# Searching the last 18 adjacency tiles of a sparse graph attention layer: other units, and a plan in two batches

## The reference

```python
h = jnp.maximum(_layernorm(x), 0.0)                  # x: 6144 x 512
h = jnp.einsum('ni,hif->hnf', h, W)                  # 8 heads of 64
s1 = jnp.einsum('hnf,hf->hn', h, a1)
s2 = jnp.einsum('hnf,hf->hn', h, a2)
scores = leaky_relu(s1[:, :, None] + s2[:, None, :], 0.2)
scores = jnp.where(adj[None] > 0, scores, -9e15)     # adj: 6144 x 6144 int32, 0 or 1
out = jnp.einsum('hnm,hmf->hnf', softmax(scores), h)
return x + elu(out as 6144 x 512)
```

## Time and profile before

| | |
|---|---|
| median of 3 runs | 793.66 us (792.19 to 800.2) |
| the profiled execution | 800.12 us, of it span 798.2 us |
| mean granted TensorE clock | 0.848 |
| DVE busy | 659.8 us, 83% |
| PE matmul busy | 570.5 us, 71% |
| ACT busy | 469.2 us, 59% |
| POOL busy | 424.6 us, 53% |
| mean DMA rate | 338 GB/s |

### The profile page before, as it was taken

The page is one execution under the profiler, slowest core; times in us unless marked ns, Lnnn a source line. Parts: engine busy times, 40 slices in busy tenths (PEclk is TensorE's granted clock), DMA queues, the critical chain, the costliest instruction groups (busy, mean ns, idle before and its releaser), DMA issues.

```text
span 798.2 us, 9153 instructions
## 1 busy us (share of the span) xinstructions
PE 570.5 (71%) x2182; PEld 407.3 (51%) x2182; DVE 659.8 (83%) x2066; ACT 469.2 (59%) x695; POOL 424.6 (53%) x804
## 2 busy tenths in 40 slices
PE   0389789898877777653777677677767669988770
PEld 0255445554444444342566465556655558766560
DVE  4659988999886767764879998999979989999871
ACT  0777797799999989324265655666455123333231
POOL 4634444443442432227666466647675776888720
PEclk9989999999998989855879879686887769997895
DMA  9999988899999999418989999999998888999986
GB/s 287 423 365 384 349 330 341 338 378 420 419 422 419 419 419 424 196 40 312 389 325 410 414 402 387 406 395 410 392 405 282 216 239 231 284 279 277 285 236 160
DMA packets 65130, 269.51 MB, mean 338 GB/s; under 512 B 12145, under 2 KB 12145, under 8 KB 52786
## 3 DMA queue, kind: packets, MB, share of 16 engines
q1 hardware_dynamic: 32098, 177.95, 55.5%
q0 software_dynamic: 26368, 78.36, 32.3%
q10 hardware_dynamic: 6608, 12.58, 4.2%
HBM read 243.49 MB, written 25.37 MB: 337 GB/s over the span
## 4 chain that ended last, share of the span: by engine, by line
DVE 20%; PE 16%; issue 10%; ACT 3%; another core or an unknown queue 3%; DMA 1%; POOL 1%; POOLq 0%; DVEq 0%; ACTq 0%
DVE nodes L1122 7%; PE psP L1260 5%; PE psP L1261 4%; DVE places L250 3%; PE psP L1267 3%; PE psP L1268 3%; DVE best L239 2%; ACT packed L229 2%; PE psC L1244 2%; DMA nodes<-table,list_column 1%; DVE agg L1134 1%; POOL nodes L959 1%; DVE to_row L1092 1%; DVE result L1142 1%
## 5 line engine op out<-in xcount | busy, mean ns | idle before, releaser
L651 PE MATMUL psH<-sb_W,normedT 128*128 128x512 f32 x384 | 222.5, 671 | 0.0
L229 ACT ACTIVATE packed<-adj_rows,eight 128x3072 uint8<-128x3072 int32 x66 | 188.5, 2856 | 3.8 <-DMA adj_rows<-in_adj_dram 3.2
L954 POOL DMA_INDIRECT nodes<-table,column x138 | 138.5, 1003 | 68.4 <-issue 39.5
L1260 PE MATMUL psP<-nodes,ident 128*128 128x256 f32 x276 | 107.8, 480 | 53.0 <-issue 40.1
L959 POOL DMA_INDIRECT nodes<-table,list_column x109 | 110.8, 1017 | 64.2 <-DVE list_column L1081 33.6
L1122 DVE TENSOR_TENSOR nodes<-nodes,psW 128x2048 f32<-128x2048 f32 (+4 forms) x66 | 138.7, 2142 | 5.1 <-ACT psW L1029 5.0
L698 POOL TENSOR_TENSOR sb_node_sum<-sb_node_sum,h_rows 128x512 f32<-128x512 f32 x48 | 61.1, 1273 | 141.4 <-ACT h_rows L616 141.4
L652 PEld LDWEIGHTS psS<-sb_Wa,normedT 128*128 128x128 f32 x384 | 78.1, 203 | 101.8 <-issue 101.8
L250 DVE FIND_INDEX8 places<-best,packed 128x8 uint32<-128x96 f32 (+6 forms) x240 | 110.4, 468 | 0.0
L239 DVE MAX8 best<-packed 128x8 f32<-128x96 f32 (+6 forms) x240 | 103.2, 463 | 4.5 <-ACT packed L229 4.5
L1261 PE MATMUL psP<-nodes,ident 128*128 128x264 f32 x276 | 104.5, 467 | 0.0
(11 more groups left out here) (177 smaller groups left out, 925.0 us busy)
## 6 DMA issues: line engine op xcount, KB each, us to landing
adj_rows<-in_adj_dram SPq DMA_DIRECT2D x66, 1536.0 KB
sb_adj_rows<-in_adj_dram SPq DMA_DIRECT2D x30, 1536.0 KB, 12.7
table<-h_rows SPq DMA_DIRECT2D x48, 260.0 KB, 8.7
sb_x_rows<-in_x_dram SPq DMA_DIRECT2D x48, 256.0 KB, 8.9
result<-in_x_dram POOLq DMA_DIRECT2D x19, 512.0 KB
out_dram<-result ACTq DMA_DIRECT2D x19, 512.0 KB
result<-in_x_dram POOLq DMA_DIRECT2D x10, 256.0 KB
out_dram<-result ACTq DMA_DIRECT2D x10, 256.0 KB
```

The lines of the kernel that those rows point to most:

```text
L229: nc.scalar.activation(words.bitcast(mybir.dt.uint8), sb["adj_rows"][buffer_of(i)][:], ACT.Square, bias=sb["eight"][:], scale=-17.0, accum ...
L651: nc.tensor.matmul(psH[:, t % 2], normedT[:, t % 2, kc], sb["W"][:, kc], start=(kc == 0), stop=(kc == KC - 1))
L954: nc.gpsimd.indirect_dma_start(out=nodes[:, node_at[u] + i * w.direct + j], out_offset=None, in_=table, in_offset=bass.IndirectOffsetOnAxi ...
L1260: nc.tensor.matmul(low, sb["ident"][:], nodes[:, n, 0:LOW], start=a, stop=False)
```

## The change

The searches move to other rounds, and the late tiles are counted and placed in two batches.

- A tile is searched whole in one round, as before, but rounds of units with ten blocks are left out. The rounds are 0 to 5, 7 to 13 and 17 to 21: tiles 30 to 35 stay where they were, tiles 36 to 42 come one round later (7 to 13), tiles 43 to 47 come four rounds later (17 to 21). ACT packs in the round before: tiles 30 to 35 as before, nothing in round 5, tile 36 in round 6, tile 37 in 7 and so on to tile 42 in round 12, nothing in 13, 14 and 15, tile 43 in round 16 up to tile 47 in round 20.
- Batch 0 is tiles 30 to 37: `count_late(0)` in round 9, `place_late(0)` at the end of round 10. Batch 1 is tiles 38 to 47: `count_late(1)` in round 22, `place_late(1)` in round 23.
- `look_up(u)` waits for the first `late_planned` where u > 12, for the second where u > 25.

```diff
     late = next(u for u, w in enumerate(UNITS) if w.tile >= EARLY)
-    COUNTED = late - 6
+    later = next(u for u, w in enumerate(UNITS) if w.tile >= SPLIT)      # SPLIT = 38
     dve_items = [(t, n) for t in range(EARLY, TILES) for n in range(2 * len(segments_of(t)))]
-    dve_round = spread_over([scan_cost(*item) for item in dve_items], COUNTED)
+
+    searchers = [u for u in range(later - 6) if UNITS[u].blocks < WIDEST]
+    dve_round = [searchers[t - EARLY] for t, _ in dve_items]
...
+    batches = [(EARLY, SPLIT, E, E + SPLIT - EARLY, scanned_in[SPLIT], late), (SPLIT, TILES, E + SPLIT - EARLY, V, later - 6, later)]
+    assert batches[0][4] <= late - 6
...
-                if u == late:
-                    pool.wait_ge(late_planned, 1)
+                for b, batch in enumerate(batches):
+                    if u == batch[5]:
+                        pool.wait_ge(late_planned, b + 1)
...
-                if u == COUNTED:
+                if u == later - 6:
                     rank_last(nc, dve, sb, TILES - 1)
-                    count_late()
-                if u == COUNTED + 1:
-                    place_late()
+                for b, batch in enumerate(batches):
+                    if u == batch[4]:
+                        count_late(b)
+                    if u == batch[4] + 1:
+                        place_late(b)
...
-                if u > COUNTED + 3:
-                    pe.wait_ge(late_planned, 1)
+                planned = sum(u > batch[4] + 3 for batch in batches)
+                if planned:
+                    pe.wait_ge(late_planned, planned)
...
-                if u == COUNTED:
-                    pe.wait_ge(late_counted, 1)
+                for b, (_, _, v0, v1, counted, _) in enumerate(batches):
+                    if u != counted:
+                        continue
+                    pe.wait_ge(late_counted, b + 1)
                     pe.wait_ge(facts_done, u + 4)
-                    nc.tensor.matmul(psC[:, 0:LV], sb["earlier"][:], listed[:], start=True, stop=True)
-                    nc.tensor.matmul(psC[:, LV:2 * LV], sb["ones"][:], listed[:], start=True, stop=True).then_inc(late_placed, 1)
+                    n, mine = v1 - v0, slice(v0 - E, v1 - E)
+                    nc.tensor.matmul(psC[:, 0:n], sb["earlier"][:], listed[:, mine], start=True, stop=True)
+                    nc.tensor.matmul(psC[:, n:2 * n], sb["ones"][:], listed[:, mine], start=True, stop=True).then_inc(late_placed, 1)
```

More of the change, by code:

```diff
@@ L42 @@
 INFO = 2 + 2 * H
+SPLIT = 38
 GROUP = 1024
@@ L849, in attend_edges @@
     E = next(k for k, v in enumerate(VISITS) if v.tile >= EARLY)
-    LV, E0 = V - E, E - FIRST["C"]
+    LV = V - E
+    batches = [(EARLY, SPLIT, E, E + SPLIT - EARLY, scanned_in[SPLIT], late), (SPLIT, TILES, E + SPLIT - EARLY, V, later - 6, later)]
+    assert batches[0][4] <= late - 6
     def ring(size):
@@ L982, in square @@
                 w = UNITS[u]
-                if u == late:
-                    act.wait_ge(late_planned, 1)
+                for b, batch in enumerate(batches):
+                    if u == batch[5]:
+                        act.wait_ge(late_planned, b + 1)
                 if u >= 2:
@@ L1151, in settle, with count_late @@
                 dve.wait_ge(late_step, steps[0])
[L1153 to L1157, removed]
+            def count_late(b):
+                t0, t1, v0, v1, _, _ = batches[b]
+                info, s, flags, mine = sb["infoC"], SLOTS["C"], sb["flags"], slice(v0 - E, v1 - E)
+                places = slice(v0 - FIRST["C"], v1 - FIRST["C"])
+                dve.wait_ge(sb["cut_step"], cut_count(t1))
+                dve.wait_ge(sb["checked"], 2 * t1)
@@ L1158, in count_late @@
                 dve.wait_ge(late_cleared, 1)
[L1159 to L1162, removed]
+                did(nc.vector.tensor_scalar(used[:, mine], info[:, places, 0:s], 0.0, None, ALU.is_gt))
+                for a, z in runs(v0, v1, lambda v: v.direct):
+                    d = VISITS[a].direct
+                    did(nc.vector.tensor_scalar(falling[:, a - E:z - E, 0:d], info[:, a - FIRST["C"]:z - FIRST["C"], 0:d],
@@ L1163, in count_late @@
                                                 -1.0, float(N + 1), ALU.mult, ALU.add))
                 settle()
-                did(nc.vector.tensor_reduce(degree[:], used[:], AX.X, ALU.add))
-                did(nc.vector.tensor_reduce(late_sums[:], sb["sums"][:, EARLY:TILES], AX.X, ALU.add))
+                did(nc.vector.tensor_reduce(degree[:, mine], used[:, mine], AX.X, ALU.add))
+                did(nc.vector.tensor_reduce(late_sums[:, mine], sb["sums"][:, t0:t1], AX.X, ALU.add))
                 settle()
-                did(nc.vector.tensor_scalar(late_sums[:], late_sums[:], -64.0 * N, None, ALU.add))
@@ L1169, in count_late @@
-                did(nc.vector.tensor_tensor(listed[:], degree[:], sb["taken"][:, E:V], ALU.subtract))
-                did(nc.vector.tensor_scalar(empty[:], degree[:], 0.0, None, ALU.is_equal))
+                did(nc.vector.tensor_scalar(late_sums[:, mine], late_sums[:, mine], -64.0 * N, None, ALU.add))
+                did(nc.vector.tensor_tensor(listed[:, mine], degree[:, mine], sb["taken"][:, v0:v1], ALU.subtract))
+                did(nc.vector.tensor_scalar(empty[:, mine], degree[:, mine], 0.0, None, ALU.is_equal))
@@ L1171, in count_late @@
                 settle()
-                nc.vector.tensor_scalar(listed[:], listed[:], 0.0, None, ALU.max).then_inc(late_counted, 1)
-                did(nc.vector.tensor_tensor(falling[:, :, 0:1], falling[:, :, 0:1], empty[:].unsqueeze(2), ALU.subtract))
-                did(nc.vector.scalar_tensor_tensor(flags[:, EARLY:TILES], degree[:], 17.0, late_sums[:],
+                nc.vector.tensor_scalar(listed[:, mine], listed[:, mine], 0.0, None, ALU.max).then_inc(late_counted, 1)
+                did(nc.vector.tensor_tensor(falling[:, mine, 0:1], falling[:, mine, 0:1], empty[:, mine].unsqueeze(2), ALU.subtract))
@@ L1175, in count_late @@
+                did(nc.vector.scalar_tensor_tensor(flags[:, t0:t1], degree[:, mine], 17.0, late_sums[:, mine],
                                                    ALU.mult, ALU.not_equal))
-                dve.wait_ge(late_counted, 1)
-                did(nc.vector.tensor_scalar(half[:], listed[:], 0.5, None, ALU.mult))
+                dve.wait_ge(late_counted, b + 1)
+                did(nc.vector.tensor_scalar(half[:, mine], listed[:, mine], 0.5, None, ALU.mult))
                 settle()
-                did(nc.vector.tensor_scalar(sb["column"][:, E:V], falling[:], float(N + 1), None, ALU.min))
@@ L1180, in count_late @@
-                did(nc.vector.tensor_tensor(sb["half_sq"][:, E:V], half[:], half[:], ALU.mult))
-            def place_late():
-                info, s, flags = sb["infoC"], SLOTS["C"], sb["flags"]
-                settle()
[L1186 to L1192, removed]
+                did(nc.vector.tensor_scalar(sb["column"][:, v0:v1], falling[:, mine], float(N + 1), None, ALU.min))
@@ new lines, in count_late, with place_late @@
+                did(nc.vector.tensor_tensor(sb["half_sq"][:, v0:v1], half[:, mine], half[:, mine], ALU.mult))
+            def place_late(b):
+                _, _, v0, v1, _, _ = batches[b]
+                info, s, flags, n = sb["infoC"], SLOTS["C"], sb["flags"], v1 - v0
+                places = slice(v0 - FIRST["C"], v1 - FIRST["C"])
+                settle()
+                dve.wait_ge(late_placed, b + 1)
+                did(nc.vector.scalar_tensor_tensor(sb["neg_centre"][:, v0:v1], psC[:, 0:n], 1.0, half[:, v0 - E:v1 - E], ALU.mult, ALU.add))
+                did(nc.vector.tensor_tensor(info[:, places, s:s + 1], psC[:, 0:n].unsqueeze(2), sb["taken"][:, v0:v1].unsqueeze(2), ALU.subtract))
+                for a, z in runs(v0, v1, lambda v: v.rest):
+                    did(nc.vector.tensor_scalar(flags[:, TILES + a:TILES + z], psC[:, n + a - v0:n + z - v0],
+                                                float(P * VISITS[a].rest), None, ALU.is_gt))
@@ L1193, in place_late @@
                 settle()
-                nc.vector.tensor_scalar(sb["neg_centre"][:, E:V], sb["neg_centre"][:, E:V], -1.0, 0.5,
+                nc.vector.tensor_scalar(sb["neg_centre"][:, v0:v1], sb["neg_centre"][:, v0:v1], -1.0, 0.5,
                                         ALU.mult, ALU.add).then_inc(late_planned, 1)
-                nc.vector.tensor_reduce(worst[:], flags[:], AX.X, ALU.max).then_inc(worst_ready, 1)
+                if v1 == V:
+                    nc.vector.tensor_reduce(worst[:], flags[:], AX.X, ALU.max).then_inc(worst_ready, 1)
```

## The result

The changed kernel takes 805.1 to 810.8 us in three runs, against a median of 794.9 us (4 runs) of the kernel before: **ratio 1.0138, 95% interval 1.0088 to 1.0189**. Repeated later with more runs it was 1.0104 (1.0058 to 1.0150). So the change costs 8 to 11 us by these two ratios, and 5 to 15 by their intervals; 8.5 were forecast. (A fourth run of the changed kernel took 1784.72 us with a granted clock of 1.0; its cause is not known, whether it took the kernel's dense fallback is not recorded, and the ratio leaves it out.) The profiled execution took 805.08 us, its span is 803.3.

What follows compares the result with a forecast made beforehand. VectorE was taken as the bound from round 3 on, with the DMA queues close behind. Terms 2.2 + 6.7 + 1.8 + 1.8 - 3.1 - 0.9 = +8.5 us on the 793.66 us median gave 802.2 us, range 794.5 to 810.

Steps and rivals of the forecast that it cites:

- the largest term: Round 10: place_late(0) at its end holds TensorE and ScalarE, making VectorE wait in round 11; 6.7 us.
- its own signs: Wrong if round 11's wait is under 3 us, gather waits appear in rounds 18-21, or rounds 14-16 end awaiting TensorE.
- Planning twice: Counting and placing in two batches adds VectorE instructions; net +2.2 us, bounds 1.0 and 3.3.
- The block in round 10: look_up(13) waits for place_late(0), ScalarE's packings queue behind, VectorE weighs late in round 11; +6.7 us, bounds 1.3 and 9.2.
- Batch 1's block "costs 1.3 as before": Round 23: placing the second batch, with no packing left, costs 1.3 us as in the kernel before.
- Short rounds: Rounds 6 and 16, packing without a search: ScalarE's second packing delays the next weighing; +1.8 us each, bounds 0 and 3.7 together.
- What goes: The gather wait at unit 16 (3.1 us) and round 15's late-packing wait (0.9 us) vanish; bounds 0 and 5.5.
- What costs nothing: rounds 17 to 21: Searches there have their packings in time: rounds of 15.1 us against about 10 us of ScalarE work; no cost.
- the queues as a rival: Rounds 17 to 21: the DMA queues become the bound, adding 4 us to the forecast, 806.2 us; chance 0.10.
- TensorE bound in units 14 to 16: Rival: ten-block rounds without a search are too short for TensorE, adding 2.8 us, 805.0 us; chance 0.12.
- Block given back: Rival: queues catch up while VectorE stands still, or short rounds cost nothing; +4.5 us, 798.2 us; chance 0.20.

Runs made afterwards that it cites:

- e2: Changed kernel with place_late of each batch moved ahead of weigh in its round (10 and 23); ratio 0.9996 to the kernel before.
- e9: Kernel before, unchanged, run again for a second profile; ratio 0.9993.
- e1: Changed kernel, as it is, run again; ratio 1.0104 to the kernel before.
- e6: Kernel before with the plan split in two batches, searches not moved, and place_late ahead of weigh; ratio 0.9976.
- e7: Kernel before with its one place_late moved ahead of weigh in round 19; ratio 0.9940.
- e3: Changed kernel with only ScalarE's packings of tiles 36, 43 and 44 moved to earlier rounds; ratio 1.0054 to the kernel before.
- e4: Changed kernel with both place_late ahead of weigh and the packings of tiles 36, 43 and 44 sooner; ratio 0.9959 to the kernel before.
- e8: Changed kernel loading only a quarter of the adjacency columns from tile 44's second half on, dense fallback switched off; ratio 0.9967 to the kernel before.
- e5: Kernel before with only the plan split in two batches, searches not moved; ratio 1.0079.
- e11: Kernel before, one plan counted in round 19, placed ahead of weigh in 20; no searches in rounds 14 and 15, tile 44 packed there; ratio 0.9903.
- e12: Kernel before, one plan counted in round 19, placed ahead of weigh; no searches in rounds 6 and 15, tile 36 packed in round 5; ratio 1.0046.

## Why the prediction was right, and where not

The time fell into the range and nearly on the point (+8.5 forecast, +8.3 and +11.0 measured), and the largest term was the right one, which e2 shows. That it came so near is in part luck. The forecast took 3.1 us of waits for gathers away and put none back, and 7.1 came in rounds 18 to 20. Busy time and waits of the later rounds differ by 15 us between the first two profiles and by 11 between e9 and e1; the 6.8 and 7.3 us that both profiles of the kernel before lost in their first rounds hid part of it. By its own signs the prediction would have been wrong twice: the wait at L1130 in round 11 was 2.25 us, under 3, and waits for gathers turned up in rounds 18 to 20.

- *Planning twice*, 2.2: 2.9 by e6 and e7, and 1.9 to 2.9 more busy time (e7 to e6, before to after). Right within what these can tell.
- *The block in round 10*, 6.7: 6.3 in the profile, and 8.6 with that of round 23 by taking both away (e2). Right, mechanism and size. I had it as one wait at the weighing; it was three, as VectorE met ScalarE's queue at the facts and at `grow` first. The sum is the same.
- *Batch 1's block "costs 1.3 as before"*: 2.2 us. The look-up that waits there, 26, has four list blocks where the kernel before had two in look-up 22, so it takes 1.89 us where look-up 22 took 1.04, both at a granted clock of 0.50, and the facts come later; a miss of 0.9. (In the kernel before, a look-up of four blocks took 0.98 us at 690.00, where TensorE had not been idle just before and the granted clock was 1.00.)
- *Short rounds*, 1.8 and 1.8: 1.64 and 1.72, and both went when the packings came sooner (e3, e4). Right.
- *What goes*, 3.1 + 0.9: both waits went, and the 1.5 of the unknown queue with them. But e9 shows 6.0 for what was 3.1 in the first profile: the term had been read from a single execution. (That its 7 us of early waits kept the term low, as I had thought, is not borne out: e9 has as many and still 6.0.)
- *What costs nothing: rounds 17 to 21.* This is the step that failed. I had put the queues as a rival with 0.10 and +4; they cost 7.1 us in the profile and 6.4 in e1, and e8 shows the loads as the cause. The figure at fault was 184 GB/s for the gathers: it came from a stretch where they had 50.7% of the engines. In rounds 17 to 20 they had 43.9% and 140 GB/s, so 2.65 MB need 18.9 us a round and not 14.4, against the 15.1 that I allowed. The rule of the Trainium skill ("DMA: Bandwidth & Descriptors", section "SWDGE vs HWDGE vs iDMA"), turns between an engine's queues, made this rival drop out by giving the gathers a half. The runs do not bear that conclusion out: there are two hardware queues beside theirs, loads with 50.2% and stores with 8.1%. And the 50.7% of busy time that seemed to agree was 7.37 of the 16.06 MB moved.
- *TensorE bound in units 14 to 16*: no wait for it in these rounds in any profile. Dropped. *Block given back*: no (e2).

So nothing here shows that the searches' new places shortened anything: the waits for gathers moved from units 6 and 14 to 16 to units 18 to 20, 6 to 8 us in either order (3.1 once). e1 less e5 prices all that is not the plan and its block at 0.0025, 2.0 us (two chips, with intervals wider than that), and the two short rounds alone are 3.4.

## What to carry to other kernels

Before a step is put into another round, read who waits for its last write and what is queued behind that waiter; here a write of 0.2 us at the wrong end of a round held TensorE 13 us and cost 6, and the same write about 10 us sooner cost VectorE no wait at all (e2). Where one engine's own work is the bound and the DMA queues run just below full, moving work can merely move the waits for transfers. The lowest ratio had one plan, placed early, and the searches left out where gathers are densest (e11), but how much of it comes from the last is not shown; a second plan cost 2 to 3 us (e6, e7). And one profile gives the waits that the program's order makes to the tenth, but those that come from queues only within some microseconds: take a second profile before a term is read from them.

## What was not expected of the hardware

Gathers lay 23.9 us between issue and use at 373 GB/s in all; with the late loads cut to a quarter their queue went from 140 to 210 GB/s, and the median from issue to landing from 15.5 to 19.9 us down to 5.3 to 5.8. VectorE lost about 7 us in the first rounds of both profiles of the kernel before and not in nine of the twelve others; of this, one wait each, 2.3 and 3.8 us, is put down to an unknown queue, and the cause is open. And e11 and e12, near twins in code and in profile (span 780.5 and 789.2 us), have medians 14 us apart.
